# Post-norm attention and LoRA feed-forward on one core: context copied out a cycle later, masks ahead of roots, a long job's matmuls one by one, four context halves moved into the cycles, a last scale on VectorE

## The reference

```python
q = jnp.dot(x, Wq).reshape(b, t, H, HD).transpose(0, 2, 1, 3)            # H 32, HD 16, t 1024
kv = jnp.dot(x, Wkv).reshape(b, t, G, 2, HD).transpose(2, 3, 0, 1, 4)    # G 8
scores = jnp.where(causal[None, None], -jnp.inf, jnp.einsum('bhqd,bhkd->bhqk', q, k))
weights = jax.nn.softmax(scores * (1.0 / HD ** 0.5), axis=-1)
ctx = jnp.einsum('bhqk,bhkd->bhqd', weights, v)
x = _layernorm(x + jnp.dot(ctx.transpose(0, 2, 1, 3).reshape(b, t, d), Wo) + bo)
h = jnp.einsum('bsd,nrd->nbsr', x, lora_A)
lora_out = jnp.einsum('nbsr,nor->bso', h, lora_B * coef)                 # coef 2 * lora_weights
x = _layernorm(x + jnp.einsum('bsd,od->bso', x, W) + bias + lora_out)
```

## Time and profile before

| | before |
|---|---|
| median of 3 runs | 368.2 us (366.19 to 368.49) |
| the profiled execution | 368.2 us, span 366.4 us |
| TensorE busy (matmuls) | 341.6 us, 93% |
| VectorE busy | 270.4 us, 74% |
| ScalarE busy | 217.0 us, 59% |
| GpSimd busy | 116.2 us, 32% |
| chain that ended last | TensorE 74%, ScalarE 9%, VectorE 5%, DMA and its queue 8% |
| granted TensorE clock, mean | 0.981 |

### The profile page before, as it was taken

One profiled execution on the slowest core, in us unless ns is written; L12 is line 12 of the kernel. 1 busy time (PEld: TensorE's weight loads), 2 busy tenths in 40 slices (PEclk: granted clock), 3 DMA queues, 4 the chain that ended last, 5 costly groups with the idle time before them and its releaser, 6 DMA issues.

```text
span 366.4 us, 6607 instructions
## 1 busy us (share of the span) xinstructions
PE 341.6 (93%) x2173; PEld 169.6 (46%) x2173; DVE 270.4 (74%) x845; ACT 217.0 (59%) x414; POOL 116.2 (32%) x225
## 2 busy tenths in 40 slices
PE   6889979999989999999999999999999999989992
PEld 3666534345434444434344443443434424338881
DVE  3338758788988988898889988898888971027663
ACT  4372125765586666774847748487485875941332
POOL 2363122433454542722122121211212113230643
PEclk9899989999999999999999999999999999998998
DMA  7959992203322110101002010000000000000002
GB/s 235 223 168 252 242 241 36 79 13 88 90 72 60 45 46 10 37 2 45 2 1 73 1 45 2 1 31 0 3 0 4 30 2 1 2 29 2 0 29 87
DMA packets 20769, 21.33 MB, mean 58 GB/s; under 512 B 6080, under 2 KB 16256, under 8 KB 20736
## 3 DMA queue, kind: packets, MB, share of 16 engines
q1 hardware_dynamic: 20736, 20.92, 21.2%
HBM read 14.68 MB, written 6.03 MB: 57 GB/s over the span
## 4 chain that ended last, share of the span: by engine, by line
PE 74%; ACT 9%; SPq 6%; DVE 5%; issue 2%; DMA 2%; POOL 1%; POOLq 0%; ACTq 0%; DVEq 0%
PE PS L1130 18%; PE PS L989 18%; PE PS L1151 16%; PE PS L967 14%; ACT PB L717 5%; SPq L481 2%; PE PS L1051 2%; PE PS L1059 2%; SPq L438 2%; PE PS L1084 1%; DMA X<-in_L_attn_x_dram 1%; PE PS L1035 1%; ACT RAW L654 1%; PE PS L1037 1%; DVE scrap L778 1%
## 5 line engine op out<-in xcount | busy, mean ns | idle before, releaser
L717 ACT ACTIVATE PB<-PS 128x512 f32<-128x512 f32 (+1 forms) x304 | 154.6, 595 | 84.5 <-PE PS L1151 84.2
L778 DVE CUSTOM_DVE_ANT_0 scrap<-PS,mask 128x128 bf16<-128x128 f32 (+3 forms) x256 | 111.1, 486 | 20.0 <-PE PS L967 19.1
L1151 PE MATMUL PS<-QS,KS 99*128 99x512 bf16 (+3 forms) x384 | 120.4, 329 | 4.2 <-ACT PB L717 3.9
L967 PE MATMUL PS<-KS,QS 96*128 96x512 bf16 (+3 forms) x384 | 109.4, 328 | 4.0 <-DVE MX L778 3.6
L595 POOL TENSOR_SCALAR_AFFINE_SELECT PB<-PB 128x256 f32<-128x256 f32 x128 | 51.3, 407 | 174.3 <-ACT PB L717 173.3
L771 DVE TENSOR_REDUCE MX<-PS 128x1 f32<-128x512 f32 x128 | 82.7, 685 | 8.6 <-PE PS L967 8.1
L1130 PE MATMUL PS<-PB,VX 128*32 128x512 f32 (+3 forms) x768 | 81.8, 498 | 3.0 <-POOL PB L595 1.6
L1151 PEld LDWEIGHTS PS<-QS,KS 99*128 99x128 bf16 x384 | 36.4, 97 | 59.4 <-ACT PB L717 35.3
L967 PEld LDWEIGHTS PS<-KS,QS 96*128 96x128 bf16 x384 | 34.3, 98 | 53.6 <-issue 22.9
L989 PE MATMUL PS<-XT,WQ 128*128 128x512 f32 x144 | 42.3, 426 | 3.6 <-DVE WQ L902 3.1
L989 PEld LDWEIGHTS PS<-XT,WQ 128*128 128x128 f32 x144 | 26.4, 197 | 9.6 <-issue 3.4
(11 more groups left out here) (76 smaller groups left out, 274.9 us busy)
## 6 DMA issues: line engine op xcount, KB each, us to landing
scr_q<-parts SPq DMA_DIRECT2D x8, 384.0 KB, 3.1
QS<-scr_q SPq DMA_DIRECT2D x16, 192.0 KB, 3.2
X<-in_L_attn_x_dram SPq DMA_DIRECT2D x8, 256.0 KB, 6.6
QS<-scr_q SPq DMA_DIRECT2D x16, 128.0 KB, 3.0
out_dram<-TC SPq DMA_DIRECT2D x8, 256.0 KB, 2.0
RAW<-in_L_attn_Wq_dram SPq DMA_DIRECT2D x1, 1024.0 KB, 8.6
QS<-scr_q SPq DMA_DIRECT2D x16, 64.0 KB, 3.1
RAW<-in_L_attn_Wo_dram SPq DMA_DIRECT2D x1, 1024.0 KB, 6.3
```

What stands on the lines that cost most here:

```text
L717: nc.scalar.activation(PB[:, cyc % NP_BUF, heads[0]:heads[-1] + 1, d * P:HT], PS[:, score_bank(e), 0:len(heads) * (HT - d * P)] .rearrange ...
L778: last = nc.vector.tensor_tensor_reduce(out=scrap[:, n % 2, (j - j0) * width:(j - j0 + 1) * width], in0=bank[:, j - j0, :], in1=mask[:, HT ...
L967: last = nc.tensor.matmul(PS[:, CHUNK_BANK[n], k * width:(k + 1) * width], QS[0:ROWS, u % SLOTS, j, qb * P:(qb + 1) * P], KS[0:ROWS, g, k0 ...
L1151: last = nc.tensor.matmul(PS[:, score_bank(e), place * width:(place + 1) * width], KS[0:NROW, u % G, kb * P:(kb + 1) * P], QS[0:NROW, u % ...
```

## The change

Five edits:
1. `evacuate(u - 1)` is no longer called behind all exponentials of the cycle with kb 0, but behind the first exponential (and a norm that stands there) of the cycle with kb 1.
2. GpSimd's root stands behind both mask pairs of its cycle, not between them.
3. A long job is issued in twelve parts, spread over the four heads and the chunks of lots 1 to 3.
4. T1a of blocks 4 to 7 is filled into cycles 86, 88, 91 and 92. Their contexts lie in `RAW[:, 4:8, :]`; `ctx_ready` is counted by the table TURNED. The tail has only T1b.
5. The last norm: VectorE adds epsilon, GpSimd makes the power alone, VectorE subtracts the mean and multiplies (L896 of the changed kernel), where ScalarE did.

```diff
+    EARLY = [("T1a", TB + i, 0) for i in range(TB)]
+    FILL.update(zip((86, 88, 91, 92), EARLY))
+    FILL = dict(sorted(FILL.items()))
...
-    TAIL = [("T1", 0), ("T1", 1), ("T2", 0), ("T2", 1), ("T1", 2), ("WO", 0), ("T1", 3), ("T2", 2), ("WO", 1),
+    TURNED = [job for c, job in FILL.items() if job[0] in ("T1a", "T1b")]
+    TURNED = [(b, int(kind == "T1b")) for kind, b, _ in TURNED] + [(TB + i, 1) for i in range(TB)]
...
+    TAIL = [("T1b", 0), ("T1b", 1), ("T2", 0), ("T1b", 2), ("T2", 1), ("WO", 0), ("T1b", 3), ("T2", 2), ("WO", 1),
...
+        CTX += [RAW[:, TB + i, :] for i in range(TB)]
...
+                if n == 2 * NT - 1:
+                    nc.gpsimd.tensor_tensor(rstd[:, s], mv[:, n % 4, 1:2], minus_half[:, 0:1], ALU.pow)\
+                        .then_inc(ln_root, 1)
+                    return
...
-                        if pair == 0 and cyc - 1 in FILL and FILL[cyc - 1][0] in ("WO", "FF"):
+                        if pair == 1 and cyc - 1 in FILL and FILL[cyc - 1][0] in ("WO", "FF"):
                             root()
...
                     if k == 0 and kind == "FF":
                         second_norm(b)
-                if kb == 0 and u:
-                    evacuate(u - 1)
+                    if k == 0 and kb == 1 and u:
+                        evacuate(u - 1)
...
+                link(nc.vector.bn_aggr(mv[:, s, :], stats[:, s, :]))
+                nc.vector.tensor_scalar_add(mv[:, s, 1:2], mv[:, s, 1:2], EPS).then_inc(ln_var, 1)
+                dve.wait_ge(out_done[1], 16 * (NT // 2 - 1))
+                dve.wait_ge(out_ready, NT - 1)
+                dve.wait_ge(ln_root, 2 * NT)
+                nc.vector.tensor_scalar(OUT[1], Y(n), mv[:, s, 0:1], rstd[:, s:s + 1], ALU.subtract, ALU.mult)\
+                    .then_inc(out_ready, 1)
...
+                if FILL[cyc][0] in LONG:
+                    for part in share(place, places, 3 * NC):
+                        fill_part(cyc, part, 3 * NC)
+                elif head % 2:
+                    fill_part(cyc, head // 2, 2)
...
+                places = REP + sum(len(lot) for lot in lots[1:])
+                place = 0
+                for j, lot in enumerate(lots):
                     for n in lot:
                         chunk_scores(n)
+                        if j:
+                            filler(cyc, 0, place, places)
+                            place += 1
                     head_scores(cyc, j)
-                    filler(cyc, j)
+                    filler(cyc, j, place, places)
+                    place += 1
```

More of the change, by code:

```diff
@@ L381, in freed @@
             if kind in ("T1a", "T1b"):
[L382 removed]
+                return ctx_ready, turned(b, int(kind == "T1b"))
             if kind in ("T2", "WO", "T3", "FF"):
@@ L931, in _ @@
                 b = B0 + i
-                if kind == "T1":
-                    for k in range(2):
-                        normalise_context(b, k, tail_bank(kind, i) + k)
+                if kind == "T1b":
+                    normalise_context(b, 1, tail_bank(kind, i))
                 else:
@@ L1098, in _, with fill_part @@
             pe.wait_ge(consts, 6)
-            def filler(cyc, head):
-                if cyc not in FILL:
-                    return
+            def fill_part(cyc, part, parts):
                 kind, b, _ = job = FILL[cyc]
-                long = kind in LONG
-                if not long and head % 2 == 0:
-                    return
-                part, parts = (head, REP) if long else (head // 2, 2)
                 if job in JOB:
@@ L1115, in filler @@
                     pe_step(kind, b, MISC_BANK[job], part, parts)
+            def filler(cyc, head, place, places):
+                if cyc not in FILL:
+                    return
+                if FILL[cyc][0] in LONG:
[3 more added lines that the diff above has]
+                    fill_part(cyc, head // 2, 2)
             def accumulate(cyc):
@@ L1180, in _ @@
                 bank = tail_bank(kind, i)
-                if kind == "T1":
-                    for k, half in enumerate(("T1a", "T1b")):
-                        if i >= 2:
-                            pe.wait_ge(ctx_ready, 2 * (b - 2) + k + 1)
-                        for part in range(3):
-                            pe_step(half, b, bank + k, part)
-                    continue
                 if kind in ("T2", "T3") and i >= 2:
```

29 lines of the change are left out of this document (17 added, 12 removed).

## The result

The changed kernel takes 375.8 us (median of 4 runs, 374.5 to 377.2) against 368.3 us: a ratio of 1.019, 95% interval 1.015 to 1.023. It is slower by 1.9%. The forecast was 373.0 us and slower. The median of these runs lies 0.3 us above the upper end of the range given (375.5). The profiled execution took 377.2 us with a span of 375.3 (before: 368.2 and 366.4).

The account below looks back on a forecast made before the run. TensorE was taken to set the time in the second half, with ScalarE having room on average. The terms -1.1 + 3.9 + 1.1 + 2.6 + 0 + 0.1 - 1.2 - 0.6 = +4.8 took 368.2 to 373.0 us, range 368.8 to 375.5.

Parts of the forecast that it names:

- copy-out, first half: First-half unit changes: accumulate waits for the later copy-out, yet starts 0.18 us earlier at each of six; -1.1 us.
- copy-out, second half: Units 9 to 14: copy-out behind exponential and 0.85 us normalisation delays accumulates by 0.74 or 0.57 us; +3.9 us.
- cycle 86: Transposes of a first half wait 0.5 us for bank 7, take 0.44, and about 0.1 remains afterwards; +1.1 us.
- cycles 88 to 93: Last unit change and transposes: +2.6 us, of which the late copy-out 1.2 and cycle 91's bank wait 1.05.
- masks: Masks ahead of the root reach only cycle 94, whose accumulate comes earlier while the last mask ends as before; 0.
- single matmuls: Spread long jobs: only two new weight loads cost 0.05 us each, and VectorE does not hold TensorE; +0.1 us.
- tail, halves gone: Tail without four first halves: first output projection 0.65 us earlier, blocks 3 and 2 give 0.55 more; -1.2 us.
- last scale: End of the kernel: one power on GpSimd, then a VectorE pass, ends at 363.4 against 363.92; -0.6 us.
- first rival: Unit changes: the copy-out's lateness is given back, boundaries cost 0; -2.4 in sum, 365.8 us; chance 0.1.
- second rival: Cycles 86 and 91: bank 7 is free in time, only copy-outs and transposes cost; 370.9 us; chance 0.27.
- the whole is wrong: Sign against the entire forecast: spreading single matmuls moves TensorE's time in a unit by over 0.2 us.
- third rival: Tail: TensorE idles more beforehand, so clock 0.50 lasts as long again; +1.8 us, 374.8 us; chance 0.15.

Follow-up runs that it names:

- p1: Kernel before with the copy-out behind the first exponential of the second cycle in units 1 to 7 only; 366.7 us, ratio 0.994.
- u1: Changed kernel with the copy-out back at its old place, behind the exponentials of the cycle with kb 0; 373.5 us, ratio 1.012.
- m1: Changed kernel with GpSimd's root again ahead of the second pair's masks; 375.0 us, ratio 1.017.
- u3: Changed kernel with the long jobs' twelve matmuls again in batches of three; 373.6 us, ratio 1.012.
- w1: m1 with six idle 512-column matmuls on zeros, read by nobody, ahead of cycle 94's accumulate; 373.9 us, ratio 1.012.
- u2: Changed kernel with the four first context halves back in the tail; 372.5 us, ratio 1.008.
- v1: Changed kernel with the copy-out, in the same later cycle, behind the first exponential but ahead of the norm; 370.7 us, ratio 1.008.
- c0: Changed kernel run again with no edit; 375.8 us, ratio 1.017 to the kernel before.
- b0: Kernel before run and profiled again with no edit; 369.4 us, ratio 1.002.
- p2: Against before: later copy-out ahead of norm except last unit change, three halves in cycles 88, 89, 92, threes, old masks, last scale on VectorE; 364.6 us, ratio 0.988.
- p3: p2 with six idle 512-column matmuls ahead of cycle 94's accumulate; 365.3 us, ratio 0.990.

## Why the prediction was right, and where it was off

The terms, as forecast and as the traces have them:

| term | forecast | measured | from |
|---|---|---|---|
| copy-out, first half | -1.1 | -1.0 to -1.16 | p1, u1 |
| copy-out, second half | +3.9 | +3.8 | u1 |
| cycle 86 | +1.1 | +1.08 | changed, cycles 84 to 86 |
| cycles 88 to 93 | +2.6 | +2.48 | changed, cycles 86 to 92 |
| masks | 0 | +0.13 | changed and m1, cycles 92 to 95 |
| single matmuls | +0.1 | +0.9 | u3 |
| tail, halves gone | -1.2 | -0.94 | w1 against u2 |
| last scale | -0.6 | -0.70 | rows below |
| a second low-clock stretch | not in the sum; rival, +1.8 | +0.82 | changed against u3, tail |
| **sum from cycle 0** | **+4.8** | **+6.4** | profile: 6.45 |
| front | none | +2.5 in this execution | same program |

**Copy-out.** The step held term by term. At unit 10 I had +0.74 and at unit 9 +0.57; the accumulates lost 0.72 and 0.54. The sign that I named, idle time ahead of those accumulates with the copy-out's end 0.14 us before their start, is in the rows above. The first rival (lateness given back) fell: the 3.8 us are still there at cycle 80, and v1 shows that they come from the norm in the queue, since they go with it. In the first half the gain at one change is 0.17 (0.18 forecast), but one sign was wrong: I expected the wait ahead of the fourth score to be gone, and it is 0.30, with 0.24 more ahead of the accumulate:

```profile
71.10 0.34 PE L1182 MATMUL PS<-QS,KS 99*128 99x384 bf16 x1 [0.30 <-ACT PB L736]
71.67 1.06 PE L1161 MATMUL PS<-PB,VX 128*32 128x512 f32 x8 [0.24 <-ACT RAW L673]
```

The exponential still stands behind the middle piece; only the copy-out has left its way.

**The last ten cycles.** The sum was nearly right (3.56 us against 3.7), its division was not, so that it fits is in part luck. The bank waits are 0.35 in cycle 86 (0.5 forecast) and 0.81 in cycle 91 (1.05), so the second rival (no bank waits) fell. The last copy-out costs 1.18 us at its accumulate, exactly as forecast, when it is alone (u2: 3.64 to 4.82), but 0.6 of that is given back by cycle 92 (4.21), since ScalarE's exponentials set the time of cycles 90 to 92. With the copy-out at its old place the halves alone cost 3.3 us (u1: 1.02 to 4.31). So the two overlap, and nearly all of the 3.6 us is the halves'. I had put 1.2 to the copy-out; on top of the halves it costs 0.3, and the halves alone 3.3 where I had 2.5.

**Single matmuls: the term that was off.** The step that failed is the count of the pairs in which a weight load is not covered: I found two new ones at 0.05 us, but spreading makes seven or eight batches where there were four, and the first matmul of each takes some 0.09 us more than those behind it. The other step, that VectorE does not hold TensorE there, failed too: by the rows above 0.23 of the 0.30 us of cycle 10 is one wait for VectorE's maxima that the batches of three do not have. It is 0.9 us in place of 0.1. The prediction named a sign by which "the whole is wrong", a unit moved by over 0.2 us by the spreading, and it came: against u3 the unit of cycles 8 to 11 loses 0.30 us. The other terms stand all the same, so as a sign for the whole it was badly chosen; it was one for this term.

**The tail and the clock.** My third rival happened in part: of the tail of the changed kernel the first output projection too runs at the low level.

```profile
339.00:341.00 2.00, 2.00 (x9) 0.50 0.16 59
...
344.00:345.00 1.00, 1.00 (x4) 0.58 0.00 0
```

TensorE was busy in all of this stretch; ahead of it, from 335 to 339, it had idled twice for masks and once for the copy-out. I priced it at +1.8, as if every matmul under it were on the path. Tails without a low stretch, with one and with two are, for this change, -2.65 (w1), -1.73 (u3) and -0.91: 0.8 to 0.9 us for each. The size was off because part of what slows down stands ahead of waits for VectorE, 0.37 and 0.54 us in w1's rows, which are gone in m1's. This stretch, which the sum put at nothing, and the single matmuls are the 1.6 us by which the sum from cycle 0 was short.

**The last scale.** The rows of the changed kernel answer to the earlier trace rows:

```profile
371.16 0.18 DVE L891 BATCH_NORM_AGGREGATE mv<-stats 128x2 f32<-128x6 f32 x1
371.38 0.15 DVE L892 TENSOR_SCALAR mv<-mv 128x1 f32<-128x1 f32 x1
371.62 0.55 POOL L593 TENSOR_TENSOR rstd<-mv,minus_half 128x1 f32<-128x1 f32 x1 [1.66 <-DVE mv L892]
372.30 0.55 DVE L896 TENSOR_SCALAR TC<-RAW,mv,rstd 128x512 f32<-128x512 f32 x1 [0.77 <-POOL rstd L593]
```

From the moments to the end it is 1.69 us against 2.39. The VectorE pass took 0.55 us, where I took 0.68 from a pass that reads PSUM. The Trainium skill ("VectorE: DVE Perf Modes", section "Mode 2×_2P — use both read ports for one tensor") has such a pass at twice the rate; by its word I had estimated 0.3 us less. The measured difference is 0.13 us, under half of the estimate. It does not show the double rate, since the two passes also differ in what they read; the measurement decides.

**The front, and what stays open.** From cycle 0 on the changed kernel is 6.4 us slower, and the medians differ by 7.5, 6.6 (c0) and 5.8 us (m1). The front's 2.5 us is not the change's: over the thirteen profiles cycle 0's accumulate starts at 57.0 to 58.1 (eight) or at 59.1 to 59.6 (five), and four of these five are the slowest run of their kernel. Why the front takes one or the other was not tried. Nor do the tail's stretches explain how the time goes with the clock: of the 19 executions of the kernel before beside c0, the fastest (364.6 us) had a mean granted clock of 0.997 and the slowest (370.9) 0.976. Nor is it settled what puts the clock down in the tail: before, b0, u1, u3 and v1 have one low stretch, changed, c0 and m1 a longer one, u2, p1, p2, p3 and w1 none, while p1 differs from before ahead of the tail only in what it gained in the first half. How the price of single matmuls divides outside cycle 10 is open as well.

## To carry to other kernels

When an instruction that others wait for is moved down an in-order queue, read what stands between its old and its new place at each of the places it is called from: the same move gave 1.1 us where the queue held an exponential and cost 3.8 where it held a norm as well. Work that fills a gap is free only if its buffer is free as well; three of the four pieces moved into the cycles cost nothing in the end where their bank had been read, or nearly, by the time that TensorE came to them, and the two that came before that took waits of 0.35 and 0.81 us. And cut a batch of matmuls into singles only where something is known to wait behind the batch.
